# First feed-forward: int8 levels in two passes, and three of six gate products on POOL

## The chip, the cores and the metric

The kernel runs on one core of a Trainium2 chip. The metric is the device time of one execution in microseconds. The engines of the core work side by side and meet only at semaphores: PE (matmuls), DVE (vector), ACT (scalar, activation functions), POOL (GpSimd) and SP, which issues the DMAs here. A few per mille can be told apart in this kernel's times: three runs of the kernel before lie between 1348.39 and 1352.10 us.

## What is computed

Two layers over x, 128 sequences of 64 steps of 256 values, with a condition vector per sequence. The change touches only the feed-forward of the first layer (h is the output of the recurrence ahead of it, 8,192 rows of 256):

```python
def _act_fake_quant(x, clip_factor):
    scale = sigmoid(clip_factor) * max(abs(x)) / 127
    return clip(round(x / scale), -128, 127) * scale

xq   = _act_fake_quant(h, clip_x[0])                 # one scale for the whole tensor
gate = xq @ _weight_fake_quant(w_gate).T             # 256 -> 704
up   = xq @ _weight_fake_quant(w_up).T
hid  = _act_fake_quant(silu(gate) * up, clip_down[0])   # needs the maximum over all rows
x    = x + hid @ _weight_fake_quant(w_down).T        # 704 -> 256
```

The second layer (attention, an MLP and a quantised linear layer) follows.

## The kernel before

The rows are worked in 16 groups of 512 rows (`NG`, `GR`). The 704 inner values are padded to six chunks of 128 (`IC`); a hidden group is thus 128 partitions by 6 x 512 f32 values. The program has four blocks, one after the other, each with an instruction list for every engine and a barrier behind it: the recurrence, `hidden`, `ffn` and the attention with all that follows.

`hidden` (tiles `a_...`) waits for the maximum of the recurrence's output, forms the scale, and then takes group after group:
- The input of a group, 128 x 1,024 f32 in `k["hs"]`, is made whole in three passes. ACT scales it and adds 1.5 x 2^23, so that it is rounded (L735, written to `rounded`); POOL clips it (L676) and takes the constant off again while writing bf16 (L681, `xq`). For the first two groups DVE clips (L785) and ACT shifts (L740). ACT issues the rounding of group g+2 after chunk 2 of group g; POOL does its two passes between its two gate products.
- PE multiplies: for each chunk two matmuls into `pg` and two into `pu` (L712), three PSUM buffers of each. Six groups have four more matmuls for the modulation of the second layer (L721).
- ACT forms silu(gate) (L754) in a ring of four tiles; it may write one when the product of four chunks before is done.
- The product with up is DVE's for chunks 0, 2, 3 and 5 (L806, straight from PSUM). For chunks 1 and 4 (`BY_POOL`) ACT copies up out of PSUM (L758) and POOL multiplies (L688).
- DVE takes the maximum over half a group at a time (L795, `half_max`): the second half of the group before after chunk 2, the first half of this one after chunk 3.
- Six of the 16 hidden groups don't fit in SBUF; SP sends them to DRAM (`SPILLED`).

`ffn` (tiles `b_...`) makes the hidden groups whole and multiplies them with the down weights. A group is three pairs of chunks, 128 x 1,024 each. ACT scales and rounds all three in place (L982). POOL clips pair 0 (L1022) and DVE pair 1 (L1045), and ACT writes both as bf16 to `hq` (L988). DVE does pair 2 in two passes, cut and floor (L1053, L1059). PE does 24 matmuls of 256 columns (L955) and, in some groups, folds the weights of the later MLP (L930 to L942). DVE scales the result out of PSUM (L1066), POOL adds x (L1031), SP stores the rows, and DVE takes their moments (L1074, L1079). `hq` has two buffers: writing group n waits until PE is through with group n-2. SP's list is in order: for each group the reload of a spilled group (1.5 MB) into the place that was just used, the load of x, the store of the group before, and a piece of the MLP weights; it waits for each step's condition before it goes on.

Of the kernel before, what the change touches and what calls it, by code (L numbers as in the profile page):

```python
# [27 lines left out]
I32 = mybir.dt.int32  # L28
ALU = mybir.AluOpType
# [3 lines left out]
P = 128  # L33
B, T, D = 128, 64, 256
C = D // P
# [550 lines left out]
def hidden(nc, dr, k):  # L586

    ctx = ExitStack()
    with ctx:
        m = Mem(nc, ctx, "a_")  # L590
        rounded = m.sb("rounded", [P, 2, C, GR])
        xq = m.sb("xq", [P, 3, C, GR], BF16)
        silu = m.sb("silu", [P, 4, GR])
        up = m.sb("up", [P, 2, GR])
# [21 lines left out]
        rounded_ready = m.sem("rounded_ready")  # L616
        clipped_first = m.sem("clipped_first")
        clipped = m.sem("clipped")
# [12 lines left out]
        BY_POOL = (1, 4)  # L631
# [38 lines left out]
        @block.gpsimd  # L670
        def _(pool):
            clear(pool, k["spent"])

            def whole(g):
                pool.wait_ge(rounded_ready, g + 1)
                pool.tensor_scalar(rounded[:, g % 2, :, :], rounded[:, g % 2, :, :], ROUND + QMAX, ROUND - QMAX - 1.0,  # L676
                                   ALU.min, ALU.max).then_inc(clipped, 1)
# [49 lines left out]
        @block.scalar  # L727
        def _(act):
            nc.scalar.activation(k["csig"][:, :], k["clips"][:, :], ACT.Sigmoid).then_inc(sig, 1)
            nc.scalar.preload_act_table(ACT.Silu)  # L730

            def round_to(g):
                if g >= 2:
                    act.wait_ge(xq_ready, g - 1)
                nc.scalar.activation(rounded[:, g % 2, :, :], k["hs"][:, g, :, :], ACT.Copy,  # L735
                                     bias=ROUND, scale=k["xinv"][:, 0:1]).then_inc(rounded_ready, 1)

            def whole(g):
                act.wait_ge(clipped_first, g + 1)
                nc.scalar.activation(xq[:, g % 3, :, :], rounded[:, g % 2, :, :], ACT.Copy, bias=-ROUND).then_inc(xq_ready, 1)  # L740

            act.wait_ge(scale_ready, 1)
            round_to(0)
            round_to(1)
            whole(0)
            whole(1)
            act.wait_ge(wx_ready, 2)
            for g in range(NG):
                for j in range(IC):
                    n = g * IC + j  # L750
                    act.wait_ge(prod_ready, n + 1)
                    if n >= 4:
                        hidden_done(act, n - 4)
                    nc.scalar.activation(silu[:, n % 4, :], pg[n % NB][:, :], ACT.Silu, scale=k["wxscale"][:, j:j + 1]).then_inc(silu_ready, 1)  # L754
                    if j in BY_POOL:
                        if g >= 1:
                            act.wait_ge(pool_hid, (g - 1) * len(BY_POOL) + BY_POOL.index(j) + 1)
                        nc.scalar.activation(up[:, BY_POOL.index(j), :], pu[n % NB][:, :], ACT.Copy,  # L758
                                             scale=k["wxscale"][:, IC + j:IC + j + 1]).then_inc(up_ready, 1)
                    if j == 2 and g + 2 < NG:  # L760
                        round_to(g + 2)

        @block.vector
        def _(dve):
# [18 lines left out]
            for g in range(EARLY):  # L783
                dve.wait_ge(rounded_ready, g + 1)
                nc.vector.tensor_scalar(rounded[:, g % 2, :, :], rounded[:, g % 2, :, :], ROUND + QMAX, ROUND - QMAX - 1.0,  # L785
                                        ALU.min, ALU.max).then_inc(clipped_first, 1)
# [11 lines left out]
            for g in range(NG):  # L798
                if g in ring and ring_use[g]:
                    dve.wait_ge(spilled[ring[g] - 3], 16 * ring_use[g])  # L800
                for j in range(IC):
# [8 lines left out]
                    if j == 3:  # L810
                        half_max(g, 0)
# [18 lines left out]
def ffn(nc, dr, k):  # L830

    ctx = ExitStack()
    with ctx:
# [28 lines left out]
        pool_clipped = m.sem("pool_clipped")  # L862
        dve_clipped = m.sem("dve_clipped")
        whole_ready = m.sem("whole_ready")
        cut_ready = m.sem("cut_ready")
        floor_ready = m.sem("floor_ready")
# [15 lines left out]
        NQ = IC // 2  # L882

# [4 lines left out]
        def _(sp):  # L888
# [18 lines left out]
            for n, g in enumerate(order):  # L907
                if n < len(SPILLED):
                    sp.wait_ge(whole_ready, 2 * (n + 1))
                    sp.wait_ge(cut_ready, n + 1)  # L910
# [14 lines left out]
        def _(pe):  # L925
# [18 lines left out]
            for n in range(NG):  # L944
                pe.wait_ge(floor_ready, n + 1)
                pe.wait_ge(whole_ready, 2 * (n + 1))
# [28 lines left out]
        def _(act):  # L975
            def pair(n, q):
                return place[order[n]][:, 2 * q:2 * q + 2, :]

            def level(n, q):
                if q == 0 and order[n] in SPILLED:  # L980
# [3 lines left out]
            def whole(n, q):  # L984
                act.wait_ge((pool_clipped, dve_clipped)[q], n + 1)
                if n >= 2 and q == 0:
                    act.wait_ge(down_ready, 2 * (n - 1))
                nc.scalar.activation(hq[:, n % 2, 2 * q:2 * q + 2, :], pair(n, q), ACT.Copy, bias=-ROUND).then_inc(whole_ready, 1)  # L988

            for n in range(NG + 1):  # L990
                if n < NG:
                    level(n, 0)
                if n >= 1:
                    whole(n - 1, 0)
                if n < NG:
                    level(n, 1)
                if n >= 1:
                    whole(n - 1, 1)
                if n < NG:
                    level(n, 2)  # L1000
# [15 lines left out]
        def _(pool):  # L1016
# [3 lines left out]
            def clip(n):  # L1020
                pool.wait_ge(level_ready, NQ * n + 1)
                pool.tensor_scalar(place[order[n]][:, 0:2, :], place[order[n]][:, 0:2, :], ROUND + QMAX, ROUND - QMAX - 1.0,  # L1022
                                   ALU.min, ALU.max).then_inc(pool_clipped, 1)
# [10 lines left out]
            for n in range(NG + 2):  # L1034
                if n < NG:
                    clip(n)
                if n >= 2:
                    add_x(n - 2, 0)
                    add_x(n - 2, 1)

        @block.vector
        def _(dve):
            def clip(n):
                dve.wait_ge(level_ready, NQ * n + 2)
                nc.vector.tensor_scalar(place[order[n]][:, 2:4, :], place[order[n]][:, 2:4, :], ROUND + QMAX, ROUND - QMAX - 1.0,  # L1045
                                        ALU.min, ALU.max).then_inc(dve_clipped, 1)

            def cut(n):

                dve.wait_ge(level_ready, NQ * n + 3)  # L1050
                if n >= 2:
                    dve.wait_ge(down_ready, 2 * (n - 1))
                nc.vector.tensor_scalar(hq[:, n % 2, 4:6, :], place[order[n]][:, 4:6, :], ROUND + QMAX, ROUND,  # L1053
                                        ALU.min, ALU.subtract).then_inc(cut_ready, 1)

            def floor(n):

                dve.wait_ge(cut_ready, n + 1)
                nc.vector.tensor_scalar(hq[:, n % 2, 4:6, :], hq[:, n % 2, 4:6, :], -QMAX - 1.0, None, ALU.max).then_inc(floor_ready, 1)  # L1059
# [24 lines left out]
            for n in range(NG + 3):  # L1084
# [5 lines left out]
                if n < NG:  # L1090
                    clip(n)
# [5 lines left out]
                if n < NG:  # L1097
                    cut(n)
# [3 lines left out]
                if n < NG:  # L1102
                    floor(n)
                if n >= 3:
# [1442 lines left out]
```

## Time and profile before

| | us |
|---|---|
| median of three runs | 1351.53 (1348.39 to 1352.10) |
| the profiled execution | 1350.4 |
| its span, first to last instruction | 1348.6 |
| `hidden`, part of the span | 131.2 (172.0 to 303.2) |
| `ffn`, part of the span | 105.4 (303.2 to 408.6) |
| attention and all behind it | 940.0 |

Over the whole span PE is busy 83%, DVE 81%, ACT 66% and POOL 46%. A busy share over a span mixes stages with different limits, so each stage is to be read by itself: first the busy time of each engine in it, then the groups of instructions by line (how many, how long one takes, what ended the idle time in front of them), then the instructions in order of time.

### The profile page before, as it was taken

To read this page: it belongs to the slowest core of one execution; us is meant where nothing else is said; L and a number is where in the kernel's file an instruction comes from. 1 tells how busy PE (TensorE), PEld (TensorE's weight loads), DVE (VectorE), ACT (ScalarE), POOL (GpSimd) and SP (SyncE) were. 2 spreads that over 40 slices of the span, in tenths; PEclk is the share of its full clock that TensorE was granted. 3 is DMA by queue.
4 is the path that set the end of the run, shared out by engine and by line. 5 is a ranking of instruction groups with operands and counts; after the bars stand their busy time and mean duration, and the time that the engine had idled before them with its cause. 6 is when DMAs were issued, how large, how long until landed. Compare 5 with 4: busy or idle time off the path is not lost.

```text
span 1348.6 us, 20238 instructions
## 1 busy us (share of the span) xinstructions
PE 1113.5 (83%) x5782; PEld 786.9 (58%) x5782; DVE 1092.8 (81%) x2486; ACT 886.0 (66%) x2374; POOL 625.4 (46%) x1075
## 2 busy tenths in 40 slices
PE   8999868866983799999999999999776776776776
PEld 7888823323442587777777777777652334444444
DVE  6887758887794578888888888888857899999995
ACT  4555478769772466666666666666688877877851
POOL 2444246645674334444444444443334566566552
PEclk9999979998996899999999999999898799989988
DMA  7334212318874433333333333433334354554423
GB/s 240 111 103 109 76 71 110 149 62 320 282 225 110 107 97 94 91 93 92 91 91 94 94 94 95 94 79 79 75 92 98 81 151 105 136 143 107 110 78 110
DMA packets 116289, 156.32 MB, mean 116 GB/s; under 512 B 9297, under 2 KB 99537, under 8 KB 114641
## 3 DMA queue, kind: packets, MB, share of 16 engines
q1 hardware_dynamic: 115632, 155.03, 41.4%
q8 instruction: 46, 0.75, 0.2%
q14 instruction: 67, 0.54, 0.1%
q10 hardware_dynamic: 544, 0.00, 0.0%
HBM read 111.22 MB, written 27.00 MB: 102 GB/s over the span
## 4 chain that ended last, share of the span: by engine, by line
issue 24%; POOL 15%; ACT 13%; DVE 10%; PE 6%; POOLq 0%; ACTq 0%; DVEq 0%
POOL t_qk L1965 5%; POOL t_u L1893 3%; POOL t_u L1898 3%; ACT t_junk L1452 2%; DVE t_bmax L1651 2%; ACT t_vbd L1509 2%; ACT t_vbd L1493 1%; DVE t_bmax L1648 1%; ACT t_y L1540 1%; ACT t_u L1443 1%; PE t_fA L2043 1%; PE t_bk L2029 1%; PE t_bk L2017 1%; DVE t_y L1614 1%; ACT t_xf L1443 1%
## 5 line engine op out<-in xcount | busy, mean ns | idle before, releaser
L2029 PEld LDWEIGHTS t_bk<-t_vbd,t_pt 128*128 128x128 f32 x1024 | 133.4, 194 | 30.0 <-issue 22.1
L2029 PE MATMUL t_bk<-t_vbd,t_pt 128*128 128x66 f32 x1024 | 131.4, 273 | 18.0 <-ACT t_pt L2147 17.0
L1397 PE MATMUL t_bk<-k_w12g,t_ut 128*128 128x512 f32 x256 | 141.8, 683 | 0.0
L2017 PE MATMUL t_bk<-t_qbd,t_kpar 128*128 128x256 f32 x512 | 136.4, 389 | 0.5 <-DMA t_qbd<-t_qt 0.5
L2017 PEld LDWEIGHTS t_bk<-t_qbd,t_kpar 128*128 128x128 f32 x512 | 93.2, 193 | 10.9 <-DMA t_qbd<-t_qt 0.9
L409 POOL TENSOR_SCALAR s_hleak<-s_hring,k_leak 128x128 f32<-128x128 f32 x128 | 48.2, 376 | 100.0 <-ACT s_hring L364 91.7
L2141 ACT ACTIVATE t_ysq<-t_y 128x768 f32<-128x768 f32 x64 | 53.8, 841 | 60.3 <-DVE t_y L2325 60.3
L1397 PEld LDWEIGHTS t_bk<-k_w12g,t_ut 128*128 128x128 f32 x256 | 57.4, 224 | 59.9 <-issue 56.9
L2043 PE MATMUL t_fA<-k_wqkv,t_ut 128*128 128x512 f32 (+1 forms) x256 | 90.9, 499 | 1.2 <-ACT t_ut L2124 1.2
L2043 PE MATMUL t_fB<-k_wqkv,t_ut 128*128 128x512 f32 (+1 forms) x256 | 88.6, 489 | 0.0
L1904 POOL TENSOR_SCALAR t_s_su<-t_s_ru 128x4 f32<-128x4 f32 x16 | 3.8, 237 | 180.9 <-ACT t_s_ru L2132 180.9
L2147 ACT ACTIVATE t_pt<-t_bk 128x512 f32<-128x512 f32 x128 | 73.7, 587 | 20.2 <-PE t_bk L2017 18.8
L277 PE MATMUL s_gsum<-s_hring,k_w0t 128*128 128x128 f32 x512 | 77.8, 295 | 8.0 <-ACT s_hring L364 3.3
L1965 POOL TENSOR_TENSOR t_qk<-t_y,t_fac 128x512 f32<-128x512 f32 x64 | 71.8, 1154 | 20.4 <-DVE t_fac L2401 20.4
L2340 DVE TENSOR_TENSOR t_o<-t_bk,t_rden 64x128 f32<-64x128 f32 x256 | 74.0, 289 | 8.5
L712 PE MATMUL a_pg<-a_xq,k_wgt 128*128 128x512 bf16 x192 | 58.7, 388 | 26.0 <-DVE k_own L806 16.0
L754 ACT ACTIVATE a_silu<-a_pg,k_wxscale 128x512 f32<-128x512 f32 x96 | 64.5, 688 | 23.7 <-PE a_pu L712 22.0
L277 PEld LDWEIGHTS s_gsum<-s_hring,k_w0t 128*128 128x128 f32 x512 | 65.8, 190 | 21.6 <-ACT s_hring L364 21.2
L2325 DVE SCALAR_TENSOR_TENSOR t_y<-t_fA,t_s_su,k_bqkv 128x768 f32<-128x768 f32 x32 | 32.6, 1017 | 50.3 <-POOL t_s_su L1904 36.9
L1393 PE MATMUL t_bk<-t_parts,t_first 128*128 128x512 bf16 x64 | 28.1, 439 | 54.5 <-DVE t_y L1614 54.5
L2043 PEld LDWEIGHTS t_fA<-k_wqkv,t_ut 128*128 128x128 f32 x256 | 48.4, 195 | 36.0 <-issue 31.9
L955 PE MATMUL b_pd<-k_wdt,b_hq 128*128 128x256 bf16 (+1 forms) x384 | 58.3, 282 | 13.1 <-ACT b_hq L988 9.1
(381 smaller groups left out, 3218.2 us busy)
## 6 DMA issues: line engine op xcount, KB each, us to landing
t_scb<-g_rows SPq DMA_DIRECT2D x64, 256.0 KB, 4.1
t_shb<-g_rows SPq DMA_DIRECT2D x64, 256.0 KB, 4.2
hidden_rows<-k_own SPq DMA_DIRECT2D x6, 1536.0 KB, 5.4
s_xrow<-in_x_dram SPq DMA_DIRECT2D x16, 512.0 KB, 3.6
k_hs<-s_hring SPq DMA_DIRECT2D x16, 512.0 KB, 3.1
b_xin<-in_x_dram SPq DMA_DIRECT2D x16, 512.0 KB, 4.6
x_rows<-b_xout SPq DMA_DIRECT2D x16, 512.0 KB, 5.2
t_xf<-x_rows SPq DMA_DIRECT2D x16, 512.0 KB, 4.6
```

What stands on the lines that cost most here:

```text
L277: last = nc.tensor.matmul(gsum[t % 2][c][:, 0:P], k["w0t"][:, kc, c * P:(c + 1) * P], hring[:, kc, (t + U - 1) % U, :], start=False, stop= ...
L712: last = nc.tensor.matmul(ps[n % NB][:, :], k["wgt"][:, v, cc, j * P:(j + 1) * P], xq[:, g % 3, cc, :], start=(cc == 0), stop=(cc == C - 1))
L754: nc.scalar.activation(silu[:, n % 4, :], pg[n % NB][:, :], ACT.Silu, scale=k["wxscale"][:, j:j + 1]).then_inc(silu_ready, 1)
L955: last = nc.tensor.matmul(pd[at % 4][:, r * D:(r + 1) * D], hq[0:w, n % 2, j, rows], k["wdt"][0:w, j, :], start=(j == 0), stop=(j == IC - 1))
L1397: last = nc.tensor.matmul(z.fW[:, j, :], z.ut[:, c, j * P:(j + 1) * P], k["w12g"][:, c, :], start=False, stop=(c == C - 1))
L1965: pool.tensor_tensor(qk[:, j, :].rearrange("p (h d) -> p h d", d=HD), y[:, j, 0:2 * D].rearrange("p (h d) -> p h d", d=HD), fac[:, 3 * j:3 ...
L2017: last = nc.tensor.matmul(bk[e % 2][:, c * 4 * T:(c + 1) * 4 * T], kpar[:, c, e, :, :].rearrange("p a t -> p (a t)"), qbd[:, c, :, e * T:( ...
L2029: last = nc.tensor.matmul(bk[2 + e % 2][:, p * VW:(p + 2) * VW], pt[:, e % 2, p * T:(p + 2) * T], vbd[:, j, h, p:p + 2, :].rearrange("p c ...
L2043: last = nc.tensor.matmul(dst[:, w0:w1], ut[:, c, j * P:(j + 1) * P], k["wqkv"][:, c, w0:w1], start=(c == 0), stop=(c == C - 1))
L2141: nc.scalar.activation(ysq[:, j % 2, :], y[:, j, :], ACT.Square).then_inc(s["ysq_ready"], 1)
L2147: nc.scalar.activation(pt[:, e % 2, :], bk[e % 2][:, :], ACT.Exp, scale=1.0 / math.sqrt(HD)).then_inc(s["exp_ready"], 1)
L2340: nc.vector.tensor_tensor(o[r, e, :].rearrange("p (q a d) -> p q a d", a=2, d=HD), ps[r, :, c, 0:2 * HD].rearrange("p q (a d) -> p q a d", ...
```

## The change

In `hidden` the three passes become two. POOL scales the input and writes it as int8 (`level`), the conversion rounding and saturating; POOL then copies it to bf16 (`whole`). ACT and DVE have no part in it any more, in the first two groups either. POOL multiplies chunks 1, 3 and 5 in place of 1 and 4, and its order in a group is product, scaling, product, copy, product. DVE is left with chunks 0, 2 and 4; its maximum over the first half now comes after chunk 4.

In `ffn` ACT scales each pair to int8, written over the front of the pair's own place (`whole_pair`), in the order 2, 1, 0, and copies pair 0 to bf16. DVE copies pair 1, POOL pair 2. The clip passes, the cut and the floor are gone. All three copies wait until PE is through with group n-2.

```diff
-        rounded = m.sb("rounded", [P, 2, C, GR])
+        xi = m.sb("xi", [P, 2, C, GR], I8)
-        up = m.sb("up", [P, 2, GR])
+        up = m.sb("up", [P, 3, GR])
-        BY_POOL = (1, 4)
+        BY_POOL = (1, 3, 5)
...
 (hidden, POOL)
+            def level(g):
+                if g >= 2:
+                    pool.wait_ge(xq_ready, g - 1)
+                pool.tensor_scalar(xi[:, g % 2, :, :], k["hs"][:, g, :, :], k["xinv"][:, 0:1], None, ALU.mult).then_inc(level_ready, 1)
             def whole(g):
-                pool.wait_ge(rounded_ready, g + 1)
-                pool.tensor_scalar(rounded[:, g % 2, :, :], rounded[:, g % 2, :, :], ROUND + QMAX, ROUND - QMAX - 1.0, ALU.min, ALU.max)...
-                pool.wait_ge(clipped, g + 1 - EARLY)
+                pool.wait_ge(level_ready, g + 1)
                 if g >= 3:
                     pool.wait_ge(prod_ready, (g - 2) * IC)
-                pool.tensor_scalar(xq[:, g % 3, :, :], rounded[:, g % 2, :, :], 1.0, -ROUND, ALU.mult, ALU.add).then_inc(xq_ready, 1)
+                pool.tensor_copy(xq[:, g % 3, :, :], xi[:, g % 2, :, :]).then_inc(xq_ready, 1)
+            pool.wait_ge(scale_ready, 1)
+            for g in range(EARLY):
+                level(g)
+                whole(g)
             for g in range(NG):
                 gate(g, 0)
                 if g + EARLY < NG:
+                    level(g + EARLY)
+                gate(g, 1)
+                if g + EARLY < NG:
                     whole(g + EARLY)
-                gate(g, 1)
+                gate(g, 2)
...
 (hidden, ACT: round_to and whole are gone; hidden, DVE: the clip of the first two groups is gone)
-                    if j == 3:
+                    if j == 4:
                         half_max(g, 0)
...
 (ffn, ACT)
-                nc.scalar.activation(pair(n, q), pair(n, q), ACT.Copy, bias=ROUND, scale=k["hinv"][:, 0:1]).then_inc(level_ready, 1)
+                nc.scalar.activation(whole_pair(n, q), pair(n, q), ACT.Copy, scale=k["hinv"][:, 0:1]).then_inc(level_ready, 1)
+            def whole(n):
+                act.wait_ge(level_ready, NQ * (n + 1))
+                if n >= 2:
+                    act.wait_ge(down_ready, 2 * (n - 1))
+                nc.scalar.activation(hq[:, n % 2, 0:2, :], whole_pair(n, 0), ACT.Copy).then_inc(act_whole, 1)
...
 (ffn, POOL, in place of clip)
+            def whole(n):
+                pool.wait_ge(level_ready, NQ * n + 1 + LEVELS.index(2))
+                if n >= 2:
+                    pool.wait_ge(down_ready, 2 * (n - 1))
+                pool.tensor_copy(hq[:, n % 2, 4:6, :], whole_pair(n, 2)).then_inc(pool_whole, 1)
...
 (ffn, DVE, in place of clip, cut and floor)
+            def whole(n):
+                dve.wait_ge(level_ready, NQ * n + 1 + LEVELS.index(1))
+                if n >= 2:
+                    dve.wait_ge(down_ready, 2 * (n - 1))
+                nc.vector.tensor_copy(hq[:, n % 2, 2:4, :], whole_pair(n, 1)).then_inc(dve_whole, 1)
```

## Rows read from the trace of the kernel before

**Rows 1.** Busy time by stretch: start:end, length, busy of each engine, clock, DMA.
```profile
172.00:303.20 131.20, 96.88 (x410) 39.35 (x410) 103.37 (x120) 99.78 (x148) 69.49 (x60) 0.94 0.25 97
303.20:408.60 105.40, 85.01 (x458) 41.61 (x458) 83.24 (x212) 85.02 (x92) 64.58 (x49) 0.90 0.79 270
```

**Rows 2.** Groups by line, 172.0 to 303.2: count | busy us, mean ns | idle before.
```profile
L754 ACT ACTIVATE a_silu<-a_pg,k_wxscale 128x512 f32<-128x512 f32 x96 | 64.5, 688 | 23.7 <-PE a_pu L712 22.0
L758 ACT ACTIVATE a_up<-a_pu,k_wxscale 128x512 f32<-128x512 f32 x32 | 21.9, 686 | 0.0
L735 ACT ACTIVATE a_rounded<-k_hs,k_xinv 128x1024 f32<-128x1024 f32 x16 | 18.1, 1138 | 0.5 <-DVE k_xinv L778 0.5
...
L795 DVE TENSOR_REDUCE a_part<-k_own 128x1 f32<-128x1536 f32 x22 | 38.3, 1743 | 0.0
L806 DVE SCALAR_TENSOR_TENSOR k_own<-a_pu,k_wxscale,a_silu 128x512 f32<-128x512 f32 x44 | 32.3, 744 | 18.4 <-ACT a_silu L754 18.4
...
L688 POOL TENSOR_TENSOR k_own<-a_up,a_silu 128x512 f32<-128x512 f32 x22 | 28.0, 1274 | 38.2 <-ACT a_up L758 38.2
L681 POOL TENSOR_SCALAR a_xq<-a_rounded 128x1024 bf16<-128x1024 f32 x14 | 14.7, 1047 | 1.2
L676 POOL TENSOR_SCALAR a_rounded<-a_rounded 128x1024 f32<-128x1024 f32 x14 | 14.6, 1041 | 8.3 <-ACT a_rounded L735 8.3
```

**Rows 3.** In order of time: start us, us, instruction; one group of `hidden`.
```profile
204.94 1.74 DVE L795 TENSOR_REDUCE a_part<-k_own 128x1 f32<-128x1536 f32 x1
205.17 1.25 ACT L754 ACTIVATE a_silu<-a_pg,k_wxscale 128x512 f32<-128x512 f32 x2
...
207.25 1.74 DVE L795 TENSOR_REDUCE a_part<-k_hs 128x1 f32<-128x1536 f32 x1
...
208.91 0.74 DVE L806 SCALAR_TENSOR_TENSOR k_hs<-a_pu,k_wxscale,a_silu 128x512 f32<-128x512 f32 x1
...
209.71 0.61 PE L712 MATMUL a_pg<-a_xq,k_wgt 128*128 128x512 bf16 x2 [0.34 <-DVE k_hs L806]
...
212.17 1.74 DVE L795 TENSOR_REDUCE a_part<-k_hs 128x1 f32<-128x1536 f32 x1
```

**Rows 4.** In order of time, the first and the last silu, and the end.
```profile
179.22 0.69 ACT L754 ACTIVATE a_silu<-a_pg,k_wxscale 128x512 f32<-128x512 f32 x1 [1.16 <-PE a_pu L712]
...
295.28 0.69 ACT L754 ACTIVATE a_silu<-a_pg,k_wxscale 128x512 f32<-128x512 f32 x1
...
300.39 0.19 DVE L769 TENSOR_REDUCE a_col<-a_part 128x1 f32<-128x32 f32 x1
```

**Rows 5.** Three lines of POOL by themselves: ns min/median/max, first and last start.
```profile
L389 POOL TENSOR_SCALAR s_wg<-s_wg,s_rscale x12: 482/483/642, 49.9 to 104.4; 128x256 f32<-128x256 f32 x12
L392 POOL TENSOR_SCALAR s_wgq<-s_wg x12: 407/422/565, 52.4 to 106.9; 128x256 bf16<-128x256 f32 x12
L1898 POOL TENSOR_TENSOR t_u<-t_u,t_shb x16: 2339/2359/2369, 422.0 to 910.5; 128x1024 f32<-128x1024 f32 x16
```

**Rows 6.** In order of time, POOL's first instruction of `ffn`, and a round of ACT.
```profile
305.28 0.20 POOL L1018 MEMSET b_ones<- 128x128 f32 x1 [8.54 <-issue]
...
308.35 1.13 ACT L982 ACTIVATE k_own<-k_own,k_hinv 128x1024 f32<-128x1024 f32 x1
...
313.36 1.13 ACT L982 ACTIVATE k_own<-k_own,k_hinv 128x1024 f32<-128x1024 f32 x1
```

**Rows 7.** In order of time, PE in `ffn`.
```profile
310.57 9.05 PE L955 MATMUL b_pd<-k_wdt,b_hq 128*128 128x256 bf16 x48 [9.14 <-ACT b_hq L988]
...
349.93 0.69 PE L930 MATMUL b_pmt<-k_ident,b_f 128*128 128x128 f32 x2 [1.78 <-DMA b_f<-in_L_cond_w_f_dram]
...
354.46 3.53 PE L955 MATMUL b_pd<-k_wdt,b_hq 128*128 128x256 bf16 x24
...
360.96 3.53 PE L955 MATMUL b_pd<-k_wdt,b_hq 128*128 128x256 bf16 x24
```

**Rows 8.** Groups by line, 303.2 to 408.6, POOL.
```profile
L1031 POOL TENSOR_TENSOR b_xout<-b_scaled,b_xin 128x512 f32<-128x512 f32 x32 | 45.3, 1431 | 29.6 <-DMA x_rows<-b_xout 22.8 <-DVE b_scaled L1066 6.5
```

More of the change, by code:

```diff
@@ L28 @@
 I32 = mybir.dt.int32
+I8 = mybir.dt.int8
 ALU = mybir.AluOpType
@@ L730, in _ @@
             nc.scalar.preload_act_table(ACT.Silu)
[L732 to L746, printed above, removed]
             act.wait_ge(wx_ready, 2)
@@ L782, in _ @@
                 nc.vector.memset(k["wxscale"][INNER - (IC - 1) * P:P, (v + 1) * IC - 1:(v + 1) * IC], 0.0).then_inc(wx_ready, 1)
[L783 to L786, printed above, removed]
             dve.wait_ge(wx_ready, 2)
@@ L861, in ffn @@
         level_ready = m.sem("level_ready")
[L862 to L866, printed above, removed]
+        act_whole = m.sem("act_whole")
+        dve_whole = m.sem("dve_whole")
+        pool_whole = m.sem("pool_whole")
         down_ready = m.sem("down_ready")
@@ L882, in ffn, with pair, whole_pair @@
         NQ = IC // 2
+        LEVELS = (2, 1, 0)
+        def pair(n, q):
+            return place[order[n]][:, 2 * q:2 * q + 2, :]
+        def whole_pair(n, q):
+            return place[order[n]][:, 2 * q, 0:GR // 2].bitcast(I8).rearrange("p (j r) -> p j r", j=2)
         def steps(ap, g):
@@ L908, in _ @@
                 if n < len(SPILLED):
-                    sp.wait_ge(whole_ready, 2 * (n + 1))
-                    sp.wait_ge(cut_ready, n + 1)
+                    sp.wait_ge(act_whole, n + 1)
+                    sp.wait_ge(dve_whole, n + 1)
+                    sp.wait_ge(pool_whole, n + 1)
                     sp.dma_start(place[SPILLED[n]], k["hid_dram"][n]).then_inc(hid_loaded[n], 16)
@@ L944, in _ @@
             for n in range(NG):
-                pe.wait_ge(floor_ready, n + 1)
-                pe.wait_ge(whole_ready, 2 * (n + 1))
+                pe.wait_ge(act_whole, n + 1)
+                pe.wait_ge(dve_whole, n + 1)
+                pe.wait_ge(pool_whole, n + 1)
                 for half in range(2):
@@ L975, in _ @@
         def _(act):
-            def pair(n, q):
-                return place[order[n]][:, 2 * q:2 * q + 2, :]
             def level(n, q):
-                if q == 0 and order[n] in SPILLED:
+                if q == LEVELS[0] and order[n] in SPILLED:
                     act.wait_ge(hid_loaded[SPILLED.index(order[n])], 16)
-                nc.scalar.activation(pair(n, q), pair(n, q), ACT.Copy, bias=ROUND, scale=k["hinv"][:, 0:1]).then_inc(level_ready, 1)
-            def whole(n, q):
-                act.wait_ge((pool_clipped, dve_clipped)[q], n + 1)
-                if n >= 2 and q == 0:
+                nc.scalar.activation(whole_pair(n, q), pair(n, q), ACT.Copy, scale=k["hinv"][:, 0:1]).then_inc(level_ready, 1)
+            def whole(n):
+                act.wait_ge(level_ready, NQ * (n + 1))
+                if n >= 2:
                     act.wait_ge(down_ready, 2 * (n - 1))
-                nc.scalar.activation(hq[:, n % 2, 2 * q:2 * q + 2, :], pair(n, q), ACT.Copy, bias=-ROUND).then_inc(whole_ready, 1)
+                nc.scalar.activation(hq[:, n % 2, 0:2, :], whole_pair(n, 0), ACT.Copy).then_inc(act_whole, 1)
             for n in range(NG + 1):
                 if n < NG:
[L992 to L1000, printed above, removed]
+                    for q in LEVELS:
+                        level(n, q)
+                    whole(n)
                 if 4 <= n < FC + 4:
@@ L1018, in _ @@
             pool.memset(ones[:, :], 1.0).then_inc(ones_ready, 1)
[L1020 to L1023, printed above, removed]
+            def whole(n):
[3 more added lines that the diff above has]
+                pool.tensor_copy(hq[:, n % 2, 4:6, :], whole_pair(n, 2)).then_inc(pool_whole, 1)
             def add_x(n, half):
@@ L1035, in _ @@
                 if n < NG:
-                    clip(n)
+                    whole(n)
                 if n >= 2:
@@ L1042, in _ @@
         def _(dve):
[L1043 to L1050, printed above, removed]
+            def whole(n):
+                dve.wait_ge(level_ready, NQ * n + 1 + LEVELS.index(1))
                 if n >= 2:
                     dve.wait_ge(down_ready, 2 * (n - 1))
[L1053 to L1059, printed above, removed]
+                nc.vector.tensor_copy(hq[:, n % 2, 2:4, :], whole_pair(n, 1)).then_inc(dve_whole, 1)
             def scale_rows(n, half):
@@ L1090, in _ @@
                 if n < NG:
-                    clip(n)
+                    whole(n)
                 if n >= 3:
@@ L1096, in _ @@
                     scale_rows(n - 2, 1)
-                if n < NG:
-                    cut(n)
                 if n >= 3:
```

11 lines of the change are left out of this document (1 added, 10 removed).

## The prediction

> **What bounds the kernel now.** I read the busy time by stage first [rows 1]. The diff touches two stages: the hidden stage (172.0 to 303.2 us, 131.2 us long) and the down stage (303.2 to 408.6 us, 105.4 us). The attention and MLP stages behind them are left alone and should only start earlier. In the hidden stage no engine is full: DVE 103.4 us, ACT 99.8, PE 96.9, POOL 69.5 of 131.2. So the stage is held by a loop through several engines, and the groups by line [rows 2] and the order of time [rows 3] must show which.
>
> A group has six chunks. DVE makes four gate products (0.744 us each) and two maxima over half a group (1.743 us each). ACT makes six silus and two up copies (0.69 each) and one rounding pass (1.138). POOL makes two products (1.274 each), a clip (1.041) and a shift (1.047). In one plain group DVE goes maximum (204.94), product, maximum (207.25), product (208.91) without a gap, and only the end of that last product, at 209.65, frees the PSUM buffers for which PE waits (it starts at 209.71). Then come the matmuls of a chunk, its silu, its product and the next maximum, at 212.17 [rows 3]. That is a closed loop of 7.23 us a group. The average is a little more: the first silu starts at 179.22 and the last at 295.28, so 116.06 us for 95 chunks, 1.222 us a chunk or 7.33 us a group [rows 4].
>
> In the down stage three things bound in turn. At first ACT does: its five passes a group come round in 5.01 us (308.35 to 313.36) [rows 6]. Then the DMA queue: PE waits 1.78 us for weights queued behind a reload of 1.5 MB, so its next group starts only at 354.46; and POOL waited 22.8 us in total for stores of x [rows 7, 8]. From 354.46 on PE runs without a gap, 6.50 us for a group that also carries the folded MLP weights (354.46 to 360.96) [rows 7].
>
> **Hidden stage, part by part.** (1) ACT loses the rounding pass (1.138) and gains a third up copy (0.686): 0.45 us less a group. Successive ACT instructions start some 0.57 us apart when nothing stops them (two silus take 1.25 together), so nine take about 5.2 us [rows 2, 3]. (2) DVE loses one product. A maximum takes a step of 1.66 (207.25 to 208.91) and a maximum with a product 2.31 (204.94 to 207.25), so a product 0.65: 3 x 0.65 + 2 x 1.66 = 5.3 us [rows 3]. (3) The loop of now is cut. DVE's two maxima are no longer followed by a product that PE waits for twice in one group: chunks 1, 3 and 5 free their PSUM by ACT's copies, so PE always has a released buffer between two of DVE's. What is late next is the fullest engine. (4) POOL gets a third product, and both its other passes stay: 3 x 1.274 + scaling + copy. PE's busy time of 96.9 us less some 8 us for the rest is at most 5.6 us a group and was never the fullest.
>
> The price of POOL's two new passes is not in this trace: no POOL row reads or writes int8. Nearest are the clip, 1.041, and the shift to bf16, 1.047, both 1,024 elements [rows 2]. A column as scale costs 0.06 more than constants (483 against 422 ns at 256 elements) [rows 5]. So the lower bound is 1.04 each (a narrower output saved nothing in the bf16 row), and as the upper one I take POOL's dearest pass over 1,024 elements, the two-source add at 2.36 [rows 5]. I take 1.10 and 1.05, since these are one-source passes with at most one operation, and the bf16 row says that another output type costs nothing. POOL then has 3.82 + 2.15 = 5.97 us a group and is the fullest engine, above DVE's 5.3. Its own order has no long gap: product, scaling, product, copy, product lie 2.3, 2.3 and 1.3 us apart, two chunks being 2 us, and a ring of four silus takes up the difference. I take 6.0 us.
>
> The clip and shift rows come to 0.86 ns an element once some 0.16 us of start is taken off. The Trainium skill (GPSIMD Engine Reference, section 3.1) has the same figure, 1.03 cycles an element for bodies of at most two operations, and adds that longer bodies are bound by issue slots, three operations a cycle. Should a conversion to int8 with rounding and saturation be such a body at two cycles, a pass would take some 1.9 us by an estimate from that page; the sum by it would be about 11 us worse for one pass. No run here shows it yet; it is what the slower rivals below would look like.
>
> The sum for this stage. Head: POOL must first clear the semaphores of the stage before. In the down stage, where it clears 25, its first instruction starts 2.1 us after the stage's start [rows 6]; here it has 47, which I put at 3.1 us, 175.1. Scaling and copy then give the first operand at 177.3, where ACT and DVE now give it at 177.1: +0.2. Middle: 95 chunks at 1.0 us from the first silu; the last two groups have no POOL passes and go at some 5.4 us, -1.2. The stage now takes 116.06 - 95 x 7.23/6 = 1.6 us more than its plain pace (a slow start, and six groups with matmuls for the modulation); a quicker pace hides less of both, and I put it at 3.8. So the last silu starts at 179.4 + 95 - 1.2 + 3.8 = 277.0, 18.3 us earlier. Tail: now a product and two maxima follow the last silu until 300.39, 5.1 us [rows 4]; then up copy, POOL product and maximum take 0.6 + 0.7 + 1.27 + 1.74 = 4.3, -0.8. Sum: **-18.9 us**.
>
> **Down stage.** ACT has three scalings and one copy in place of three and two: 5.01 less a step of 0.95, plus some 0.15 because the copy now waits for its own scalings: 4.2 us. DVE loses its clip, cut and floor for one copy; at 0.7 to 1.13 us it has about 4 us a group. POOL's clip becomes a copy, 1.05 (bounds as above), and with two additions it has some 3.8. In all the first operand is there about 0.9 us sooner (PE now starts at 310.57) [rows 7], and four groups later ACT is 0.9 + 4 x 0.8 = 4 us ahead. From there PE and the DMA queue give the pace. The queue's traffic is unchanged and was nearly full, so part of the 4 us is lost again; but the reloads are issued 1 to 3 us sooner, and the stall of 1.78 may shrink. New is that POOL's copy waits for PE to be through with the group two before, and behind it on POOL stand the two additions of x, and behind those the store that SP issues: x goes out 1 to 1.8 us later after each PE group. In a PE-bound stretch that costs nothing; where the queue bounds it takes back about 1 us. Bounds: 0 and -7; I take **-3.5 us**, half way, since both ends are reasoned from the same queue.
>
> Together -22.4 us. The profiled execution took 1350.4 us (span 1348.6 and 1.8 around), the median of the runs is 1351.5. 1350.4 - 22.4 = **1328 us**; its own range, from -15 to -30, is 1320 to 1335.
>
> **Rivals.** (A) Coupling stays. Now the fullest engine has 6.3 us in 7.24, a factor of 1.15. If POOL's 5.97 is stretched alike to 6.87, each of the 14 full groups is 0.87 slower than the forecast's 6.0: +12.2, less 1 or so because a slower pace hides more of the start: 1339 (1335 to 1342). For it: six groups with extra matmuls, and a POOL that must never idle; against it: what stretched the loop was DVE's product after a maximum, which is gone.
> (B) One int8 pass is dear, up to 2.36. POOL then has up to 7.28 a group, 14 x 1.28 = 17.9 us above the forecast less 2 for the start: 1344 at the end of it, 1338 where the pass takes 1.9. What remains is the gain of the last two groups, which have no such pass, and of the down stage.
> (C) Both are dear: the one that ends slower. POOL has 3.82 + 4.72 = 8.54 us a group and everything waits for it: 14 x 1.21 = +16.9, head +2.6, last two groups and tail -4.7, down stage about 0: 1365. It decides from about 2.0 us a pass on; below that the change still gains. For it: no row shows int8 on POOL; against it: the two rows with bf16 output [rows 2, 5].
> (D) The change does its part in the first stage and not in the second, the queue eating all: 1332, within the forecast's own range.
>
> **Chances.** Forecast with (D) 0.62, (A) 0.15, (B) 0.12, (C) 0.08, and 0.03 for other losses (contention of POOL with DVE in the down stage, where additions stretch from 1.27 to 1.43 on average) [rows 8]. A measurement of this kernel tells about 0.3% (4 us) from no change. Faster: 0.62 + 0.15 + most of (B), 0.85; same 0.06; slower 0.09. The range 1318 to 1345 takes in the forecast, (A) and nearly all of (B).
>
> **What would show it.** In the profile after: POOL's scaling and copy at 1.04 to 1.1 us in the groups by line; POOL busy close to all of the hidden stage; silus 1.0 us apart and the last at about 277; no PE wait of over a microsecond for a product of DVE; the stage's end at 284. In the down stage PE's first group at 309.5 less those 19 us, gapless 6.50 us groups from about the seventh on, and its length 102 in place of 105.4. A POOL pass above 2 us makes it wrong; so would silus over 1.15 us apart with POOL idle.

## The result and the profile after

| | us |
|---|---|
| predicted | 1328 (1318 to 1345) |
| kernel before, median of 9 runs | 1350.95 (1348.39 to 1352.10) |
| changed kernel, median of 9 runs | 1355.92 (1354.02 to 1356.64) |
| ratio, 95% interval | 1.0038 (1.0028 to 1.0048) |

The changed kernel is 5 us slower where 22 us less were forecast. Its profiled execution took 1356.5 us, with a span of 1354.7. Below, a stage's length is the time between the first instructions that ACT executes in it and in the next stage.

| length, us | before | changed | forecast |
|---|---|---|---|
| before the hidden stage | 172.0 | 173.8 | 172.0 |
| hidden stage | 131.2 | 133.5 | 112.3 |
| down stage | 105.4 | 105.4 | 101.9 |
| all behind it | 940.0 | 942.1 | 940.0 |

The first and last lines hold no changed instruction. By the profiles the changed kernel is 28.5 us over its forecast: 21.1 in the hidden stage, 3.5 in the down stage and 3.9 outside them. The busy time by stretch, of the changed kernel (start:end, length, busy of PE, PEld, DVE, ACT and POOL, granted clock, DMA share, GB/s):

```profile
173.79:307.24 133.45, 100.39 (x402) 38.45 (x410) 91.44 (x102) 89.24 (x146) 120.36 (x80) 0.93 0.25 95
307.24:412.64 105.40, 85.56 (x458) 41.65 (x458) 60.93 (x180) 70.63 (x76) 62.29 (x49) 0.89 0.79 269
```

Against [rows 1], DVE fell from 103.4 to 91.4 and ACT from 99.8 to 89.2 as meant, but POOL went from 69.5 to 120.4: it is busy nine tenths of the stage, and the forecast's POOL, gapless as it was to be, should have needed some 96. The groups by line say which instruction it is (count | busy us, mean ns | idle before):

```profile
L676 POOL TENSOR_SCALAR a_xi<-k_hs,k_xinv 128x1024 int8<-128x1024 f32 x16 | 45.8, 2863 | 9.3 <-issue 9.3
L689 POOL TENSOR_TENSOR k_own<-a_up,a_silu 128x512 f32<-128x512 f32 x33 | 42.1, 1288 | 1.8 <-ACT a_up L751 1.8
...
L682 POOL CAST a_xq<-a_xi 128x1024 bf16<-128x1024 int8 x16 | 16.9, 1055 | 0.1
...
L747 ACT ACTIVATE a_silu<-a_pg,k_wxscale 128x512 f32<-128x512 f32 x96 | 64.6, 691 | 38.1 <-POOL k_own L689 15.6 <-PE a_pu L720 14.8 <-POOL k_hs L689 7.5
```

The copy out of int8 costs 1.055 us, as forecast (1.05). The scaling into int8 costs 2.863 us where 1.10 was taken, more than the upper bound of 2.36. And ACT, which before waited for PE alone [rows 2], now waits 23.1 us (15.6 + 7.5) for POOL's products to free its silu and up buffers. POOL's order in one group, the same kernel (start us, us, instruction):

```profile
240.24 2.86 POOL L676 TENSOR_SCALAR a_xi<-k_hs,k_xinv 128x1024 int8<-128x1024 f32 x1
243.05 1.28 POOL L689 TENSOR_TENSOR k_own<-a_up,a_silu 128x512 f32<-128x512 f32 x1
244.26 1.05 POOL L682 CAST a_xq<-a_xi 128x1024 bf16<-128x1024 int8 x1
245.26 2.51 POOL L689 TENSOR_TENSOR k_own<-a_up,a_silu 128x512 f32<-128x512 f32 x2
247.74 2.85 POOL L676 TENSOR_SCALAR a_xi<-k_hs,k_xinv 128x1024 int8<-128x1024 f32 x1
```

There is no gap, and a group takes 247.74 - 240.24 = 7.50 us, against 7.23 for a plain group of the old loop and 7.33 on average [rows 3, 4]. The old loop is gone, and a full POOL at the same pace stands in its place. The first silu and the last:

```profile
183.53 0.69 ACT L747 ACTIVATE a_silu<-a_pg,k_wxscale 128x512 f32<-128x512 f32 x1 [8.23 <-PE a_pu L720]
...
299.31 1.27 ACT L747 ACTIVATE a_silu<-a_pg,k_wxscale 128x512 f32<-128x512 f32 x2
```

From the stage's start to the first silu it is now 9.74 us, against 7.21: the first operand now waits for POOL's semaphores, one dear scaling and a copy. The time from the first to the last silu hardly moved (116.4 us to the second of the last pair, which starts 0.57 behind the first, against 116.06).

In the down stage PE goes like this (in order of time):

```profile
312.35 7.85 PE L949 MATMUL b_pd<-k_wdt,b_hq 128*128 128x256 bf16 x40 [6.92 <-DVE b_hq L1033]
...
329.09 3.52 PE L949 MATMUL b_pd<-k_wdt,b_hq 128*128 128x256 bf16 x24
336.05 0.69 PE L923 MATMUL b_pmt<-k_ident,b_f 128*128 128x128 f32 x2 [3.44 <-DMA b_f<-in_L_cond_w_f_dram]
336.53 3.62 PE L932 MATMUL b_pw<-b_ff 128*128 128x512 f32 x4
340.08 1.50 PE L935 MATMUL b_pb<-b_ff,b_b1c 128*1 128x512 f32 x2
341.51 3.53 PE L949 MATMUL b_pd<-k_wdt,b_hq 128*128 128x256 bf16 x24
...
409.65 0.69 PE L964 MATMUL b_pmt<-k_ident,b_mvt 128*64 128x64 f32 x8 [7.12 <-DVE b_mvt L1053]
```

Counted from the stage's start (307.24), the first group starts at +5.1, where before it was 310.57 - 303.23 = +7.3 [rows 7]: 2.2 us gained, more than the forecast's 0.9. The fifth (329.09) is at +21.85, where before it was at +27.6. Then PE waits 3.44 us for the weights of the folded MLP, and the four matmuls behind the wait take 3.62 us where the same four take 1.88 a group later. SP had issued the piece (`b_f`) at 327.09, just behind the reload of a hidden group and the load and the store of x:

```profile
324.94 0.44 SPq L904 DMA_DIRECT2D k_own<-hidden_rows  x1
...
327.09 0.43 SPq L893 DMA_DIRECT2D b_f<-in_L_cond_w_f_dram  x1
```

PE could go on at 336.05, 9 us after the issue. The stretches of that time give the granted clock, the last but two columns:

```profile
336.00:340.10 4.10, 4.05 (x7) 1.52 (x8) 2.92 (x6) 4.07 (x6) 3.75 (x3) 0.50 0.98 411
...
348.00:352.00 4.00, 3.54 (x25) 2.00 (x24) 0.95 (x7) 1.94 (x3) 0.00 (x0) 1.00 0.99 347
```

PE had stood still, and it was granted 0.50, the lower of its two levels (1.2 of 2.4 GHz). The kernel before paid some of this too: behind its wait of 1.78 us [rows 7] the same four matmuls took 3.17 us, at 0.63 over the stretch from 350 to 354. By the last group PE is still 2.8 us ahead (+91.8 against +94.5 from the stage's start), and that is given back behind it. POOL's additions for the last two groups both wait for stores of x:

```profile
401.67 2.48 POOL L1017 TENSOR_TENSOR b_xout<-b_scaled,b_xin 128x512 f32<-128x512 f32 x2 [1.67 <-DMA x_rows<-b_xout]
...
406.04 2.48 POOL L1017 TENSOR_TENSOR b_xout<-b_scaled,b_xin 128x512 f32<-128x512 f32 x2 [1.90 <-DMA x_rows<-b_xout]
```

Before, only the last did (1.84 us). So PE's last matmuls wait 7.12 us for the statistics (5.38 before), and the stage is as long as it was.

### The profile page after: what moved, and what is told of

The parts are those of the page before. It is cut to its first block, busy times and chain, and to the rows that moved or that the text cites. A ratio compares the mean times of both kernels' runs of the same rounds, so it can differ in the third digit from the quotient of the medians.

```text
span 1354.7 us, 20192 instructions
## 1 busy us (share of the span) xinstructions
PE 1110.5 (82%) x5760; PEld 783.2 (58%) x5782; DVE 1062.2 (78%) x2436; ACT 861.1 (64%) x2356; POOL 673.8 (50%) x1095
## 4 chain that ended last, share of the span: by engine, by line
issue 24%; POOL 15%; ACT 13%; DVE 9%; PE 7%; POOLq 0%; ACTq 0%; DVEq 0%
POOL t_qk L1934 5%; POOL t_u L1862 3%; POOL t_u L1867 3%; ACT t_junk L1421 2%; DVE t_bmax L1620 2%; ACT t_vbd L1478 2%; ACT t_vbd L1462 1%; PE t_bk L1366 1%; ACT t_y L1509 1%; DVE t_bmax L1617 1%; PE t_fB L1387 1%; PE t_fA L2012 1%; ACT t_u L1412 1%; ACT t_xf L1433 1%; PE t_bk L1998 1%
## 5 line engine op out<-in xcount | busy, mean ns | idle before, releaser
L747 ACT ACTIVATE a_silu<-a_pg,k_wxscale 128x512 f32<-128x512 f32 x96 | 64.6, 691 | 38.1 <-POOL k_own L689 15.6
L278 PEld LDWEIGHTS s_gsum<-s_hring,k_w0t 128*128 128x128 f32 x512 | 66.6, 192 | 21.1 <-ACT s_hring L365 20.7
L288 PE MATMUL s_gsum<-s_xt,k_w0t 128*128 128x128 f32 x512 | 69.1, 279 | 0.2 <-DVE s_xt L424 0.2
L1387 PE MATMUL t_fB<-k_wmt,t_qbd 128*128 128x256 f32 x256 | 68.6, 403 | 0.0
```

The lines of the kernel that those rows point to most:

```text
L278: last = nc.tensor.matmul(gsum[t % 2][c][:, 0:P], k["w0t"][:, kc, c * P:(c + 1) * P], hring[:, kc, (t + U - 1) % U, :], start=False, stop= ...
L288: nc.tensor.matmul(gsum[t % 2][c][:, 0:P], k["w0t"][:, C + kc, c * P:(c + 1) * P], xt[:, t % 4, kc, :], start=(kc == 0), stop=False)
L1387: last = nc.tensor.matmul(z.fM[:, j * D:(j + 1) * D], z.xdt[:, c, j * P:(j + 1) * P], k["wmt"][:, c, :], start=False, stop=(c == C - 1))
```

## The experiments

Theory 1: the price of the scaling makes POOL the bound of the hidden stage; in the down stage the gain exists but the DMA queue gives it back. Rivals: the loss is in the down stage; the loop stays whatever POOL costs. What a kernel differs by is told against the changed kernel unless another is named. A ratio is always to the kernel before, measured alongside; a stage's length is that of the profiled execution.

**One stage at a time** (no diff: one of the two functions is that of the kernel before).

> The hidden stage of the changed kernel with the down stage of the kernel before. Theory 1 (the price): POOL's scaling to int8 takes 2.86 us where 1.10 was forecast, so POOL asks for 2.86 + 1.06 + 3 x 1.29 = 7.78 us a group, more than the old loop's 7.33, and the stage is 2 us longer: 133 to 134 us from its first instruction to the next stage's, the kernel 2 to 4 us over the kernel before (ratio 1.001 to 1.003). Rival (the down stage lost it): this kernel alone is at or under the time before, and the down stage's int8 passes cost the 5 us.

> The hidden stage of the kernel before with the down stage of the changed kernel. Theory 1: the down stage by itself gains nothing, since what it gains in its head is given back at its DMA queue and in its tail: within 1.5 us of the kernel before, ratio 0.999 to 1.001, the stage 105 us long. The step of the prediction said 3.5 us less (0.9974). Rival (the down stage lost it): over 1.002.

Measured: hidden_only 1354.59 us, ratio 1.0027 (1.0015 to 1.0039); hidden stage 133.5 us. down_only 1350.16 us, ratio 0.9989 (0.9972 to 1.0006); down stage 104.4. The loss is in the hidden stage; the down stage's effect lies between a gain of 3.8 us and a loss of 0.8. The stage explains 2.2 us of hidden_only's 3.9, and 2.2 is inside the interval (2.0 to 5.3 us).

**Is it the type?**

```
-        xi = m.sb("xi", [P, 2, C, GR], I8)
+        xi = m.sb("xi", [P, 2, C, GR], BF16)          # level_bf16
+        xi = m.sb("xi", [P, 2, C, GR], mybir.dt.int16) # level_i16
```

> The changed kernel with POOL's scaling written as bf16 in place of int8, every other instruction and wait as it is; this leaves out the rounding and the clipping to whole levels. Theory 1 (the integer output is what costs): the scaling falls from 2.86 us to 1.04 to 1.10, POOL's group to 6.0, the hidden stage to 113 to 117 us and the kernel to 1336 to 1340 us. Rival (the loop through PE, ACT and DVE holds the stage whatever POOL's price): the scaling falls, but a group stays at or over 7.0 us and the kernel over 1346 us. Rival (the price is in the operation or its contention, not in the output's type): the scaling stays over 2 us.

> The changed kernel with the scaling's output as int16, twice the bytes of int8; this leaves out the clipping to 8 bits. If the conversion to an integer costs, the scaling takes 2.8 us as with int8 and the time is that of the changed kernel; if it is the output of one byte, the scaling takes 1.04 to 1.10 and the time is that with bf16. A value between says that both have a part.

The scaling in level_bf16, then in level_i16, from the groups by line:

```profile
L676 POOL TENSOR_SCALAR a_xi<-k_hs,k_xinv 128x1024 bf16<-128x1024 f32 x16 | 45.6, 2850 | 9.3 <-issue 9.3
```

```profile
L676 POOL TENSOR_SCALAR a_xi<-k_hs,k_xinv 128x1024 int16<-128x1024 f32 x16 | 45.6, 2848 | 9.3 <-issue 9.3
```

level_bf16 took 1355.65 us, ratio 1.0037 (1.0024 to 1.0049), level_i16 1357.39 (one run). My theory falls in this point: the conversion to int8 costs nothing that shows (0.013 us). 2.85 us is the price of the instruction with each of these three outputs. So the prediction's worry (int8) was groundless, and its calm ("another output type costs nothing") was right and did not help. What distinguishes the instruction from POOL's clip (1.041) and shift (1.047) [rows 2] is that it has one operation and no second operand, and that its scale is a column.

**Is it the form?**

```
-  pool.tensor_scalar(xi..., k["hs"]..., k["xinv"][:, 0:1], None, ALU.mult)
+  pool.tensor_scalar(xi..., k["hs"]..., k["xinv"][:, 0:1], 0.0, ALU.mult, ALU.add)   # two_op
+  pool.tensor_scalar(xi..., k["hs"]..., 16.0, None, ALU.mult)                        # const_one
```

> The changed kernel with one difference: POOL's scaling carries a second operation, an addition of 0.0, so it computes the same as before. Theory 2 (the form): what costs 2.86 us is the one-operation form with no second operand, since the output's type had no part in it, while every row of POOL at 0.86 ns an element has two operations. Then the scaling falls to 1.05 to 1.15, POOL's group to 6.05 us, the hidden stage to 110 to 117 us and the kernel to 1330 to 1338 us (ratio 0.985 to 0.990). Rival (the source or the column operand): the scaling stays at 2.8 us and the kernel at 1355. Rival (the loop): the scaling falls but the groups stay over 7.0 us and the kernel over 1346.

> The changed kernel with a constant 16.0 in place of the computed scale, still one operation; the levels of the first pass are then wrong. If the missing second operation alone makes the price, the scaling stays at 2.8 us. If the column operand makes it, it falls to 1.04. Between them: both have a part.

two_op, groups by line:

```profile
L689 POOL TENSOR_TENSOR k_own<-a_up,a_silu 128x512 f32<-128x512 f32 x33 | 42.0, 1272 | 10.3 <-ACT a_up L751 10.3
...
L676 POOL TENSOR_SCALAR a_xi<-k_hs,k_xinv 128x1024 int8<-128x1024 f32 x16 | 17.9, 1118 | 9.3 <-issue 9.3
L682 POOL CAST a_xq<-a_xi 128x1024 bf16<-128x1024 int8 x16 | 16.6, 1036 | 0.1
```

const_one, the scaling by itself (ns min/median/max):

```profile
L676 POOL TENSOR_SCALAR a_xi<-k_hs x16: 2770/2771/2790, 175.8 to 285.5; 128x1024 int8<-128x1024 f32 x16
```

With an addition of 0.0 the scaling takes 1.118 us in place of 2.863. A constant in place of the column takes off only 0.09, and the kernel gains nothing by it: POOL's copies then stand 7.64 us apart where they stood 7.50, the hidden stage is 135.4 us, and the one run took 1355.73; where the extra time between the instructions comes from is open. So the missing second operation is the price: 1.65 to 1.75 us on 1,024 elements, and doing more work is 2.5 times as fast. Why the form costs this, no run here shows. two_op takes 1338.64 us, ratio 0.9917 (0.9901 to 0.9933), 17.3 us under the changed kernel (16.3 by the two ratios); its hidden stage is 117.6 us. Both are 0.6 us outside what I expected (110 to 117 and at most 1338). Its busy time by stretch, hidden and down stage:

```profile
172.09:289.66 117.57, 95.29 (x402) 40.49 (x410) 91.59 (x102) 89.35 (x146) 93.37 (x80) 0.94 0.27 108
289.66:394.69 105.03, 84.53 (x458) 41.05 (x458) 60.94 (x180) 70.63 (x77) 61.87 (x49) 0.91 0.79 271
```

And POOL in it, from one scaling to the next in a plain group:

```profile
196.53 1.12 POOL L676 TENSOR_SCALAR a_xi<-k_hs,k_xinv 128x1024 int8<-128x1024 f32 x1
197.61 1.27 POOL L689 TENSOR_TENSOR k_own<-a_up,a_silu 128x512 f32<-128x512 f32 x1
...
201.36 1.27 POOL L689 TENSOR_TENSOR k_hs<-a_up,a_silu 128x512 f32<-128x512 f32 x1 [0.27 <-ACT a_up L751]
202.60 1.12 POOL L676 TENSOR_SCALAR a_xi<-k_hs,k_xinv 128x1024 int8<-128x1024 f32 x1
```

202.60 - 196.53 = 6.07 us, the 6.0 of the prediction. But only the first groups are plain. From 205 us on POOL's copies stand 6.64 and 6.41 us apart in turn, with gaps of 0.8 and 0.6 us in POOL before a product, where a plain group has 0.27. In every second of these groups PE puts 1.03 us of modulation matmuls between the chunks. I take it that the loop through PE and ACT is then a little longer than POOL's work; no run leaves these matmuls out.

**Which part of the hidden stage's change pays?** Against two_op:

```
-        BY_POOL = (1, 3, 5)
+        BY_POOL = (1, 4)
...
-                gate(g, 2)
...
-                    if j == 4:
+                    if j == 3:
                         half_max(g, 0)
```

> two_op with two of the six gate products on POOL and four on DVE, as in the kernel before: only the cheaper two passes are left of the hidden stage's change. The prediction's step 3 (the loop through DVE's maxima and products sets the pace until DVE loses a product): groups stay 7.2 us apart, hidden stage 129 to 132 us, kernel 1349 to 1353. Rival (the passes taken from ACT are the gain): groups at 6.5 us or less and the kernel at 1340 or under.

Measured 1348.32 us, ratio 0.9984 (0.9974 to 0.9993), no more than the down stage gives (103.8 us for 105.4). Hidden stage 131.4 us. POOL's copies in the order of time:

```profile
201.17 1.04 POOL L682 CAST a_xq<-a_xi 128x1024 bf16<-128x1024 int8 x1
...
208.40 1.03 POOL L682 CAST a_xq<-a_xi 128x1024 bf16<-128x1024 int8 x1
```

7.23 us a group, the old loop exactly, with ACT busy 84.2 us of 131 (99.8 before) and POOL 73.9. Taking the passes away from ACT gave nothing; what breaks the loop is the fourth product moved off DVE, together with the maximum behind chunk 4 that goes with it. The two were only moved together, so which of them does it isn't shown. Step 3 of the prediction, which rests on both, is right.

**The down stage.** Against down_only (down_f1), and against the kernel before (before_f1), the load of one weight piece is issued first:

```
+            def load_f1(f): ...              # the first load of load_f, moved out
             for n, g in enumerate(order):
+                if n < FC:
+                    load_f1(n)
                 if n < len(SPILLED):
                     ...                      # the reload of a group, 1.5 MB
```

and in down_addfirst, against down_only, POOL's order is turned:

```
                 if n >= 2:
                     add_x(n - 2, 0)
                 if n < NG:
                     whole(n)
                 if n >= 2:
                     add_x(n - 2, 1)
```

> Hidden stage of before, down stage of the change, and SP issues the load of the MLP's first-factor piece ahead of the reload of a group instead of behind it. Theory 3 (the queue takes back what the passes gave): PE's wait of 3.4 us for that piece goes, the groups from the fifth on start 3 us sooner, and the kernel is 2 to 4 us under down_only (1346 to 1348 us). Rival (the reload is what the groups need next): PE waits for a reloaded group or x instead and the time is that of down_only, within 1 us.

> The kernel before with the load of the first-factor piece ahead of the reload, nothing else. If the change's down stage has a real gain that only the queue hid, this kernel gains less than down_f1 does: PE's wait of 1.78 us goes and the ACT-paced first groups stay, 1347.5 to 1350 us. Rival (the order of the loads is the whole gain, the cheaper passes give nothing): the same 1345 us as down_f1.

> Hidden stage of before, down stage of the change, with POOL's order turned: the first addition of x of the group two before stands ahead of the copy, the second behind it. Theory 3: the copy's new wait for PE delays x's additions and stores by up to 1.3 us a group, and the tail of the stage (PE's end to the stage's end, 10 us where it was 7.4) is part of that: the stage ends 0 to 2.5 us sooner. Rival (the x stores wait in the DMA queue whatever POOL does): the same as down_only within 1 us.

| | us | ratio | down stage, us |
|---|---|---|---|
| down_only | 1350.16 | 0.9989 (0.9972 to 1.0006) | 104.4 |
| down_f1 | 1345.27 | 0.9951 (0.9933 to 0.9968) | 98.1 |
| before_f1 | 1347.48 | 0.9982 (0.9969 to 0.9994) | 104.5 |
| down_addfirst | 1348.91 | 0.9986 (0.9968 to 1.0005) | 102.7 |

PE in down_only, and then in down_f1 over the same groups:

```profile
333.49 0.69 PE L937 MATMUL b_pmt<-k_ident,b_f 128*128 128x128 f32 x2 [4.64 <-DMA b_f<-in_L_cond_w_f_dram]
333.97 3.24 PE L946 MATMUL b_pw<-b_ff 128*128 128x512 f32 x4
...
338.10 3.53 PE L963 MATMUL b_pd<-k_wdt,b_hq 128*128 128x256 bf16 x24
```

```profile
326.14 3.52 PE L967 MATMUL b_pd<-k_wdt,b_hq 128*128 128x256 bf16 x24
329.87 0.41 PE L941 MATMUL b_pmt<-k_ident,b_f 128*128 128x128 f32 x2 [0.21 <-ACT b_ff L1009]
330.12 1.88 PE L950 MATMUL b_pw<-b_ff 128*128 128x512 f32 x4
...
332.88 3.52 PE L967 MATMUL b_pd<-k_wdt,b_hq 128*128 128x256 bf16 x24
...
339.38 3.53 PE L967 MATMUL b_pd<-k_wdt,b_hq 128*128 128x256 bf16 x24
```

With the piece in front, the wait of 4.6 us is gone, the MLP matmuls behind it take 1.88 us from the first on, and the groups follow each other in 6.5 us. That is the queue's share. The piece was moved ahead of the load and the store of x too, so how much of it the 1.5 MB alone had isn't separated. before_f1 shows the other half: without the cheaper passes the same reordering leaves the stage at 104.5. PE's first group waits 9.14 us for ACT as before, and the next ones start 5.0 us apart, ACT's round. Its eighth group does start 2.7 us sooner than in the kernel before, but behind it POOL's additions wait 3.9 and 3.1 us for stores of x, and its last starts only 0.8 sooner. In the profiled executions the stage is 1.0 us shorter with the passes alone, 0.9 with the order of the loads alone and 7.3 with both. By the ratios it is 1.5 us (not clear of noise), 2.4 and 6.6 for the kernel, and these intervals don't rule out a plain sum. down_addfirst is not told apart from down_only by its times. Its last matmuls wait 6.76 us for the statistics against 6.78, so the tail is not the copy's doing. Its stage is 1.7 us shorter in the one profile, within what was expected, and shorter ahead of the tail; with times from 1342 to 1355 us that settles nothing, and whether the copy's wait costs anything stays open.

**Both repairs together.**

> The changed kernel with both repairs: the 0.0 added as second operation of POOL's scaling, and the first-factor piece loaded ahead of the reload. If the two gains are independent (two_op 17.3 us under the changed kernel, down_f1 4.9 under down_only) the kernel takes 1331 to 1335 us, hidden stage 117 to 118, down stage 98 to 99. Rival (the phase of the DMA queue undoes one of them): 1336 or more.

> As the kernel called best, but the scaling to int8 is ACT's (its one-operation form took 1.14 us in the down stage) and POOL keeps the copy and three products. ACT has nine instructions 0.57 us apart and one of 1.14, 6.3 us a group, POOL 4.8. If the pace is that of the fullest engine, groups lie 6.3 to 6.5 us apart as in two_op and the kernel is within 2 us of best. Rival (POOL's fill is what still couples the loop): groups at 6.1 or less throughout and 3 us or more under best.

The kernel called best takes 1332.51 us, ratio 0.9855 (0.9831 to 0.9879), hidden stage 118.2 and down stage 100.3 (98 to 99 expected): 6.1 us under two_op, so the gains add up within the noise of four runs. act_level_f1, where ACT makes the scaling

```
+                nc.scalar.activation(xi[:, g % 2, :, :], k["hs"][:, g, :, :], ACT.Copy,
+                                     scale=k["xinv"][:, 0:1]).then_inc(level_ready, 1)
```

after its third chunk, takes 1329.92 us, ratio 0.9847 (0.9832 to 0.9862), hidden stage 118.8. ACT's rows in it:

```profile
202.36 1.16 ACT L734 ACTIVATE a_xi<-k_hs,k_xinv 128x1024 int8<-128x1024 f32 x1
...
208.99 1.16 ACT L734 ACTIVATE a_xi<-k_hs,k_xinv 128x1024 int8<-128x1024 f32 x1
```

A group takes 6.63 us here, and 6.5 to 6.6 all through the stage, though POOL is busy for only 76 us of it. So freeing POOL doesn't speed up the stage. ACT is now the fullest engine, busy 104 us of 119; that it sets the pace is argued from this, not tested. The groups are a little slower than the 6.3 to 6.5 expected. The intervals of the two kernels overlap; either beats the kernel before by 1.5%, and the changed one by a little more.

## Why the prediction was wrong, point by point

- **The price of POOL's scaling** is the step that failed: taken at 1.10, bounded by 1.04 and 2.36, measured 2.863. Undone alone it brings back 17.3 us (16.3 by the ratios) of the 28 between forecast and result. The choice rested on "one-source passes with at most one operation". But every row it leaned on, clip, shift and the column-scaled row [rows 2, 5], has two operations, and the case in hand had one. The upper bound was the dearest row of another kind of instruction and bounded nothing. The Trainium skill (GPSIMD Engine Reference, section 3.1) gives all bodies of at most two operations one price, 1.03 cycles an element. two_op's row at 1.118 us fits that (1,024 elements at the 0.86 ns of the prediction are 0.88 us, without the start); const_one's 2.771 us does not, and the measurement decides. The conversion to int8, from which the prediction built a price of 1.9 us, costs nothing here (2.863 against 2.850).
- **Rival (B)** named the mechanism (a dear pass fills POOL), but its price ended at 2.36 and 7.28 us a group. At 2.863, POOL's steps add up to 7.50 a group. By the prediction's own way of counting, 14 x (7.50 - 6.0) = 21 us are lost, and 2.5 us in the head where 0.2 stood, less 2 for the start as in (B); measured, the stage came out 21.1 us over the forecast. (B) put the dearness in int8, though, and that was not it: two_op writes int8 too.
- **Steps 1 to 4 given the price** hold for the plain groups: DVE and ACT lost what was said, the loop is cut by moving the product and the maximum (two_products), and a plain group takes 6.07 us for 6.0.
- **The middle of the hidden stage** was mis-sized by 4.6 us. In two_op the silus run from 180.08 to 282.3, 102.2 us where 97.6 were forecast: the allowance of 3.8 for the start and the modulated groups should have been 8.4, because ten groups go at 6.4 to 6.6. The head is +0.8 instead of +0.2 (POOL's first scaling starts 3.7 us into the stage, not 3.1), the tail -0.6 instead of -0.8. Together the stage gives 13.7 us, not 18.9.
- **The down stage**, taken at -3.5 half way between 0 and -7, gave 0.0 in the changed kernel and 1.0 in down_only. The gain at its start was real (2.2 us at the first group, 5.8 by the fifth). The step that failed is "the stall of 1.78 may shrink": it grew to 3.44, because a PE that is ahead asks earlier for a piece that is queued behind 1.5 MB. With the slow matmuls behind the stall this takes about half of the 5.8 us, and the longer wait for the statistics at the end takes the other 2.8. Rival (D) had this stage right, the stores of x being in the same queue. Whether the wait of POOL's copy for PE costs the 1 us of the prediction is open (down_addfirst). The copy itself, priced at 1.05, takes 1.33 to 1.53 us in this stage.
- **Beside the stages** the first part came out 1.8 us longer and the last 2.1, with the same instructions. Over all kernels here the first part is 172.0 to 173.8 us and the last 937 to 943, so one profile can't assign 2 us of either to the change. What moves them stays open.
- **Slips in the working that decided nothing.** The hidden stage's terms add up to 19.1 us, not 18.9: the 0.2 of the head is in the 18.3 already. Rival (A)'s 6.3 us for the fullest engine is in no row; DVE's steps give 5.9 a group and its busy time 6.5. (B)'s 7.28 should be 7.23 with the copy at 1.05. The 0.16 us of start taken off the clip and shift is in no row either: the shift at 256 and at 1,024 elements (0.422 and 1.047 us) gives 0.81 ns an element and 0.21 us of start.

## What to carry to other kernels

Before an instruction is priced from a neighbour's row, compare its form: number of operations and kinds of operands, not only engine, type and size. On POOL, write a single scaling as two operations (times the scale, plus 0.0), or give it to ACT. And when an engine is made to arrive earlier at a shared DMA queue, look at what it will ask for first and put that ahead of the bulk reload; here the stage lost 7.3 us by both changes and about 1 by either alone.

## What was unexpected of the hardware

- POOL's tensor_scalar with one operation takes 2.77 to 2.86 us for 128 x 1024 elements, and 1.118 us with a second operation of +0.0, with an int8 output in both. In the one-operation form bf16, int16 and int8 outputs cost 2.850, 2.848 and 2.863.
- POOL's plain copies from int8 and int16 to bf16 take 1.04 to 1.06 us in the hidden stage, so they don't fall under it. In the down stage of the changed kernel the same copy from int8 takes 1.33 us on average from one place and 1.53 from the other (`k_own`, `k_hs`), while x's additions went from 1.43 to 1.28; what stretches it wasn't tested. ACT's scaling to int8 takes 1.14 to 1.16 us, also in a form with no second operation.
- A wait of 3.44 us of PE was followed by six matmuls at 3.62 + 1.50 us instead of 1.88 + 1.02, at a granted clock of 0.50 in the first 4 us instead of 1.00: 2.2 us came on top of the wait. Behind a wait of 1.78 us, in the kernel before, four of them took 3.17 us.
